# One alignment stage of an eight-part network: where the moves of the path are computed, and how its arrays travel

## The reference, cut to what matters

```python
def align_one(small, large):            # small: 77 x 256 context, large: 1024 x 256 normed tokens
    D = sqrt(max(|a|^2 + |b|^2 - 2 a.b, 0))       # 77 x 1024
    R = dtw_cost(D)     # R[i,j] = D[i,j] + min(R[i-1,j], R[i,j-1], R[i-1,j-1])
    # walk back from (76, 1023): at each cell take the least of diagonal, up, left
    # (in this order on a tie), until (0, 0)
    i_idx, j_idx, valid = backtrack(R)
    return zeros(1024, 256).at[j_idx].add(small[i_idx] * valid)
x = x + align(ctx, layernorm(x))
x = x + slots(layernorm(x))             # the stage behind it
```

## Time and the profile before

| | us |
|---|---|
| median of 3 runs | 4073.38 |
| lowest and highest | 4072.11, 4077.62 |
| the profiled execution, its own time | 4080.33 |
| its span, first to last instruction | 4078.5 |
| TensorE busy (share of the span) | 3017.4 (74%) |
| VectorE busy | 2092.9 (51%) |
| ScalarE busy | 1485.4 (36%) |
| GpSimd busy | 1015.0 (25%) |
| mean granted TensorE clock | 0.862 of full speed |

### The profile page before, as it was taken

How to read it: one execution, slowest core, us unless ns; L and a number is a source line. 1 busy time by engine, 2 the same in 40 slices (tenths; PEclk the granted TensorE clock), 3 DMA queues, 4 the chain that set the end, 5 groups by cost and what they waited for, 6 DMA issues and landing times. The chain is left out here.

```text
span 4078.5 us, 41019 instructions
## 1 busy us (share of the span) xinstructions
PE 3017.4 (74%) x14054; PEld 1775.1 (44%) x14054; DVE 2092.9 (51%) x3702; ACT 1485.4 (36%) x2034; POOL 1015.0 (25%) x593
## 2 busy tenths in 40 slices
PE   3999999999974577199567699998279520059979
PEld 1555555455534444189444333333279410024344
DVE  3655555565513354277454588776267444731270
ACT  2344444444433223256233255555156210012240
POOL 1355556565632211300311100000411312001100
PEclk7899999999986789599789699999589765579999
DMA  2000000000003300256100000000156224110050
GB/s 88 5 6 1 5 5 5 1 4 5 2 1 120 96 11 1 90 191 226 52 11 1 11 4 5 2 3 2 55 204 220 80 24 52 9 26 31 27 201 21
DMA packets 94303, 194.15 MB, mean 48 GB/s; under 512 B 30937, under 2 KB 67417, under 8 KB 86090
## 3 DMA queue, kind: packets, MB, share of 16 engines
q1 hardware_dynamic: 74730, 83.01, 7.6%
q0 software_dynamic: 16464, 103.18, 7.5%
q10 hardware_dynamic: 2960, 6.03, 0.4%
HBM read 149.16 MB, written 42.76 MB: 47 GB/s over the span
## 5 line engine op out<-in xcount | busy, mean ns | idle before, releaser
L602 POOL TENSOR_TENSOR A_key_sums<-A_key_sums,A_probs 128x1024 f32<-128x1024 f32 (+1 forms) x224 | 526.8, 2370 | 227.0 <-ACT A_probs L495 227.0
L495 ACT ACTIVATE A_probs<-A_banks 128x512 f32<-128x512 f32 (+1 forms) x576 | 329.4, 597 | 389.5 <-PE A_banks L415 387.1
L545 DVE TENSOR_REDUCE A_part_max<-A_banks 128x1 f32<-128x367 f32 x768 | 354.0, 530 | 156.9 <-PE A_banks L336 155.5
L1750 DVE TENSOR_REDUCE F_part_max<-F_banks 128x1 f32<-128x512 f32 x512 | 325.0, 683 | 59.6 <-PE F_banks L1603 56.8
L1696 ACT ACTIVATE F_probs<-F_banks 128x1024 f32<-128x1024 f32 x256 | 248.1, 1022 | 237.9 <-PE F_banks L1649 237.7
L364 PE MATMUL A_banks<-A_probs,A_v_tok 128*64 128x512 f32 x1152 | 278.7, 605 | 0.0
L413 PE MATMUL A_banks<-A_q_one,A_k_one 128*128 128x512 f32 (+1 forms) x576 | 258.3, 448 | 26.2 <-ACT A_probs L495 23.1
L336 PE MATMUL A_banks<-A_k_one,A_q_one 128*128 128x368 f32 x768 | 230.0, 382 | 6.8 <-ACT A_v_tok L475 6.4
L2064 PE MATMUL G_banks<-G_path,G_ctx_rows 77*128 77x512 f32 x16 | 14.0, 1071 | 293.9 <-DMA G_ctx_rows<-in_G_ctx_rows 293.9
L415 PE MATMUL A_banks<-A_q_two,A_k_two 128*128 128x512 f32 (+1 forms) x576 | 228.2, 396 | 0.0
L167 POOL TENSOR_SCALAR F_r<-F_r,F_ln_w 128x512 f32<-128x512 f32 x16 | 28.8, 1813 | 660.5 <-DVE F_r L132 660.5
(11 more groups left out here) (536 smaller groups left out, 6330.1 us busy)
## 6 DMA issues: line engine op xcount, KB each, us to landing
H_w<-in_H_w SPq DMA_DIRECT2D x11, 1024.0 KB, 4.8
moe_in<-A_zeros ACTq DMA_DIRECT2D x1, 5888.0 KB, 17.3
D_tile_in<-moe_in SPq DMA_DIRECT2D x23, 256.0 KB, 5.3
moe_out<-D_z SPq DMA_DIRECT2D x23, 256.0 KB, 4.9
F_tile_in<-moe_in SPq DMA_DIRECT2D x23, 256.0 KB, 5.2
moe_out<-F_z SPq DMA_DIRECT2D x23, 256.0 KB, 4.9
H_phi<-in_H_w SPq DMA_DIRECT2D x5, 1024.0 KB, 4.7
B_tile_in<-moe_in SPq DMA_DIRECT2D x15, 256.0 KB, 2.9
```

The lines of the kernel that those rows point to most:

```text
L495: act.activation(probs[0:kw, j, kt % RING, blk * BLK:(blk + 1) * BLK], ps[0:kw, half % 3, :], ACT.Exp, scale=1.0 / 8.0).then_inc(s["exp_re ...
L545: dve.tensor_reduce(part_max[:, i // 3, i % 3:i % 3 + 1], ps[:, MAX_BANKS[i % 3], 0:PIECE], AX.X, ALU.max).then_inc(s["piece_max"], 1)
L602: pool.tensor_tensor(key_sums[0:kw, j, :], before, probs[0:kw, j, kt % RING, :], ALU.add).then_inc(s["summed"], 1)
L1750: op = dve.tensor_reduce(part_max[:, maximum_at(hd, qt), kb:kb + 1], bank, AX.X, ALU.max)
```

## The change

The distances are stored and fetched for each sequence as soon as its two blocks are ready; each skewed fetch is cut in a first quarter of the slots (FIRST = 23) and the rest, with semaphores of their own. `G_start` is loaded early. Only `cost_dram` is padded, with a `fill` of 15 x 1024 in place of 15 x 4096. TensorE multiplies the context and the tokens ahead of the norm of the tokens.

Blocks G2 to G5 become one block. The totals stay in SBUF, and the moves are computed from them in the wave layout, [64, 92 x 64], by five VectorE instructions and two shuffles that fetch the neighbour lane's edge. The path is stored in two parts for each sequence (the later 46 slots, LATE, when they are done, the earlier 46 at the end) and loaded straight for each sequence. The context rows are loaded at the block's start and split in a rounded part and a rest, both fp32r, so each product in fp32 becomes two accumulating products in fp32r. GpSimd presets the path array and one slot of each move array.

```diff
-    def skewed(a, b):
-        return bass.AP(a.tensor, b * ROWS * S + PAD * W, [[S - W, CK], [S, SLOTS], [1, W]])
+    FIRST = SLOTS // 4
+    LATE = SLOTS // 2
+    def skewed(a, b, first=0, last=SLOTS):
+        return bass.AP(a.tensor, b * ROWS * S + PAD * W + first * S, [[S - W, CK], [S, last - first], [1, W]])
...
 # G1
-            pool.memset(fill[:, 0], BIG).then_inc(s["filled"], 1)
-            pool.memset(fill[:, 1], 0.0).then_inc(s["filled"], 1)
+                pool.memset(fill[:, :], BIG).then_inc(s["filled"], 1)
...
-            sp.wait_ge(s["cost_ready"], NBLK)
-            sp.dma_start(straight(cost_dram), cost[:, :].rearrange("r (b n) -> r b n", b=B)).then_inc(s["stored"], 16)
-            sp.wait_ge(s["stored"], count + 16)
+                sp.wait_ge(s["wave_filled"], 1)
+                sp.dma_start(total[:, 0, :], t["G_start"]).then_inc(start_loaded, 16)
+                sp.wait_ge(s["wave_filled"], 2)
+                sp.wait_ge(s["padded"], 16 * 2 * B)
+                for b in range(B):
+                    sp.wait_ge(s["cost_ready"], (b + 1) * NBLK // B)
+                    sp.dma_start(straight(cost_dram, b), cost[:, b * S:(b + 1) * S]).then_inc(s["stored"], 16)
+                    sp.wait_ge(s["stored"], 16 * (b + 1))
+                    lanes = slice(32 * b, 32 * b + CK)
+                    sp.dma_start(cost_wave[lanes, 0:FIRST], skewed(cost_dram, b, 0, FIRST)).then_inc(first_loaded, 16)
+                    sp.dma_start(cost_wave[lanes, FIRST:], skewed(cost_dram, b, FIRST)).then_inc(rest_loaded, 16)
 # one block for what were G2 to G5
+            move = sc.sb("move", [LANES, 2, SLOTS + 1, W + 1])
+            left = sc.sb("left", [LANES, SLOTS + 1, W + 1])
+            path = sc.sb("path", [LANES, SLOTS + 1, W + 1])
+            path_rows = sc.sb("path_rows", [CTX, B, S], F32R)
...
+            @block.sync
+            def _(sp):
+                sp.dma_start(ctx_rows[:, :, :], t["G_ctx_rows"]).then_inc(s["ctx_loaded"], 16)
+                sp.wait_ge(s["path_zeroed"], 1)
+                sp.dma_start(path[:, SLOTS, :], t["G_end"]).then_inc(s["end_loaded"], 16)
+                for first, last in ((LATE, SLOTS), (0, LATE)):
+                    sp.wait_ge(s["path_ready"], SLOTS - first)
+                    for b in range(B):
+                        sp.dma_start(skewed(path_dram, b, first, last), path[32 * b:32 * b + CK, first:last, 0:W])\
+                          .then_inc(path_stored[b], 16)
+                for b in range(B):
+                    sp.wait_ge(path_stored[b], 32)
+                    sp.dma_start(path_rows[:, b, :].bitcast(F32), straight(path_dram, b)).then_inc(path_loaded[b], 16)
+            @block.scalar
+            def _(act):
+                act.wait_ge(s["ctx_loaded"], 16)
+                act.activation(ctx_hi[:, :, :], ctx_rows[:, :, :], ACT.Copy).then_inc(s["hi_ready"], 1)
+            @block.vector
+            def _(dve):
+                dve.wait_ge(s["hi_ready"], 1)
+                dve.tensor_tensor(ctx_lo[:, :, :], ctx_rows[:, :, :], ctx_hi[:, :, :].bitcast(F32), ALU.subtract)\
+                   .then_inc(s["lo_ready"], 1)
+                dve.wait_ge(start_loaded, 16)
+                dve.wait_ge(first_loaded, 16 * B)
+                for n in range(SLOTS):
+                    if n == FIRST:
+                        dve.wait_ge(rest_loaded, 16 * B)
...                   # the three instructions of a slot as before
+                c_up, c_diag, c_left = total[:, 0:SLOTS, 1:], total[:, 0:SLOTS, 0:W], total[:, 1:, 0:W]
+                up, diag, to_left = move[:, 0, 0:SLOTS, 0:W], move[:, 1, 0:SLOTS, 0:W], left[:, 0:SLOTS, 0:W]
+                step(dve.tensor_tensor(least[:, :, :], c_up, c_left, ALU.min))
+                step(dve.tensor_tensor(diag, c_diag, least[:, :, :], ALU.is_le))
+                step(dve.tensor_tensor(up, c_up, c_left, ALU.is_le))
+                step(dve.scalar_tensor_tensor(out=to_left, in0=diag, scalar=0.0, in1=up, op0=ALU.is_equal, op1=ALU.is_gt))
+                step(dve.tensor_tensor(up, up, diag, ALU.is_gt))
+                step(dve.stream_shuffle(move[:, 1, 0:SLOTS, W], move[:, 1, 1:SLOTS + 1, 0], from_right))
+                step(dve.stream_shuffle(left[:, 0:SLOTS, W], left[:, 1:SLOTS + 1, 0], from_right))
...                   # 92 slots backward, four instructions each as before, then x + ps four times
+            @block.tensor
+            def _(pe):
+                pe.wait_ge(s["lo_ready"], 1)
+                for n in range(NBLK):
+                    b, blk = divmod(n, S // BLK)
+                    if blk == 0:
+                        pe.wait_ge(path_loaded[b], 16)
+                    for c in range(C):
+                        for k, part in enumerate((ctx_hi, ctx_lo)):
+                            mm = pe.matmul(ps[:, C * n + c, :], part[:, b, c * P:(c + 1) * P],
+                                           path_rows[:, b, blk * BLK:(blk + 1) * BLK], start=k == 0, stop=k == 1)
+                    mm.then_inc(s["out_ps"], 1)
```

More of the change, by code:

```diff
@@ L1823, in align_stage @@
[L1823 to L1843, removed]
-            pool.memset(fill[:, 0], BIG).then_inc(s["filled"], 1)
-            pool.memset(fill[:, 1], 0.0).then_inc(s["filled"], 1)
[L1846 to L1864, removed]
-                for c in range(C):
[L1866 to L1908, removed]
-            sp.wait_ge(s["cost_ready"], NBLK)
-            sp.dma_start(straight(cost_dram), cost[:, :].rearrange("r (b n) -> r b n", b=B)).then_inc(s["stored"], 16)
-            sp.wait_ge(s["stored"], count + 16)
@@ L1914, in align_stage @@
[L1914 to L1958, removed]
-        up = least
-        diag, left = (sc.sb(n, [CTX, B, S + 1]) for n in ("diag", "left"))
-        filled, back_filled, loaded, dve_step, stored = (
-            sc.sem(n) for n in "filled back_filled loaded dve_step stored".split())
-        block = stack.enter_context(nc.Block())
-        @block.gpsimd
-        def _(pool):
-            for a in (here, over):
-                pool.memset(a[:, :, 0:1], BIG).then_inc(filled, 1)
-            pool.memset(over[0:1, :, 1:], BIG).then_inc(filled, 1)
-            for a in (diag, left):
-                pool.memset(a[:, :, S:S + 1], 0.0).then_inc(filled, 1)
-            for a in (move[:, 0], move[:, 1], left_moves[:, :, :], path_wave[:, :, :]):
-                pool.memset(a, 0.0).then_inc(back_filled, 1)
-            pool.wait_ge(back_filled, 4)
-            pool.memset(move[:, 0, SLOTS, :], 1.0).then_inc(back_filled, 1)
-            pool.wait_ge(back_filled, 5)
-        @block.sync
-        def _(sp):
-            sp.dma_start(here[:, :, 1:], straight(total_dram)).then_inc(loaded, 16)
-            sp.dma_start(over[1:, :, 1:], straight(total_dram)[0:CTX - 1]).then_inc(loaded, 16)
-            sp.wait_ge(dve_step, 6)
-            for a, dst in ((up[:, :, 0:S], 0), (diag[:, :, 1:], 1), (left[:, :, 1:], 2)):
-                sp.dma_start(straight(move_dram[dst]), a).then_inc(stored, 16)
-            sp.wait_ge(stored, 48)
-        @block.vector
-        def _(dve):
-            step = chain(dve, dve_step)
-            dve.wait_ge(filled, 5)
-            dve.wait_ge(loaded, 32)
-            c_up, c_diag, c_left = over[:, :, 1:], over[:, :, 0:S], here[:, :, 0:S]
-            step(dve.tensor_tensor(least[:, :, :], c_up, c_left, ALU.min))
-            step(dve.tensor_tensor(diag[:, :, 0:S], c_diag, least[:, :, :], ALU.is_le))
-            step(dve.tensor_tensor(least[:, :, :], c_up, c_left, ALU.is_le))
-            step(dve.tensor_scalar(not_diag[:, :, :], diag[:, :, 0:S], -1.0, 1.0, ALU.mult, ALU.add))
-            step(dve.tensor_tensor(up[:, :, 0:S], least[:, :, :], not_diag[:, :, :], ALU.mult))
-            step(dve.tensor_tensor(left[:, :, 0:S], not_diag[:, :, :], up[:, :, 0:S], ALU.subtract))
@@ L2003, in align_stage @@
-    with ExitStack() as stack:
-        sc = Scope(nc, stack, "G4")
-        left, path = left_moves, path_wave
-        below = sc.sb("below", [LANES, 2, W])
-        enter = sc.sb("enter", [LANES, W])
-        loaded, edge_ready, below_ready, enter_ready, row_ready, stored = (
-            sc.sem(n) for n in "loaded edge_ready below_ready enter_ready row_ready stored".split())
-        from_right = [CK] + list(range(CK - 1)) + list(range(CK, 32))
-        block = stack.enter_context(nc.Block())
-        @block.sync
-        def _(sp):
-            for b in range(B):
-                for a, src in zip((move[:, 0], move[:, 1], left), move_dram):
-                    sp.dma_start(a[32 * b:32 * b + CK, 0:SLOTS], skewed(src, b)).then_inc(loaded, 16)
-            sp.dma_start(path[:, SLOTS, :], t["G_end"]).then_inc(loaded, 16)
-            sp.wait_ge(row_ready, SLOTS)
-            for b in range(B):
-                sp.dma_start(skewed(path_dram, b), path[32 * b:32 * b + CK, 0:SLOTS, 0:W]).then_inc(stored, 16)
-            sp.wait_ge(stored, 32)
-        @block.vector
-        def _(dve):
```

(42 more changed lines are left out.)

129 lines of the change are left out of this document (added).

## The result

The changed kernel takes 3998.33 us (median of 4 runs, 3996.7 to 4002.21) against 4072.74 (4 runs beside it): 74.4 us less, ratio 0.9817 with a 95% interval of 0.98 to 0.9834. The forecast was 4001.

The account below looks back on a forecast made before the run. One engine or transfer at a time was taken as the path, mostly transfer waits between passes. Savings 4.2 + 53.3 + 16.6 - 1.5 = 72.6 us from 4073.38 give 4001 us, range 3989 to 4013.

Parts of the forecast that it names:

- Middle: Between the forward and backward passes: transfers and waits go, five instructions and two shuffles come; 53.3 us sooner.
- the bounds: Between the passes, each shuffle of 92 columns: from 0.14 us if columns are free to 12.9 us; 0.25 taken.
- Head: First fill to forward pass: earlier distances and fetches by sequence, start waiting for context rows; 4.2 us sooner.
- Tail: Last backward scan to last add: half stores, loads by sequence and fp32r products; 16.6 us sooner.
- Backward pass: Backward slots: the first half's store runs under the last 46 slots without slowing them; 0 us.
- Given back: nH, behind the stage: less TensorE work in front leaves more of it at half clock; 1.5 us lost.
- The dearer moves: Rival, between the passes: shuffles cost by the column (+25 us) or runs of 64 at half rate (+31); 4026 to 4032; 10%.
- The head that isn't late: Rival, head: context rows land past the fetches at 3316, pass starts near 3317.3; 4.3 us better, 3997; 8%.
- The clock behind the stage: Rival, H stage products: the clock stays low, making the kernel slower than before; up to 4226 us; 3%.

Follow-up runs that it names:

- three runs: Changed kernel with context rows loaded first in G1, with each fetch uncut, and with both edits; heads 28.8, 32.9 and 32.0 us against 33.7.
- fetch_at_end: Changed kernel with both sequences' distances stored when all are ready, then both fetched, uncut; head 40.2 us against 33.7.
- the two uncut runs: Changed kernel with each sequence's fetch in one transfer, context rows loaded where the change put them or first in G1; heads 32.9 and 32.0 us.
- path_at_once: Changed kernel with each sequence's path stored in one transfer after the last slot; tail 21.3 us against 16.8.
- fp32_products: Changed kernel with the last products in fp32 from the context rows, copy and subtraction kept unused; tail 23.5 us against 16.8.
- warm_clock: Changed kernel with 21 extra TensorE products during the last backward slots and the path's store and load; tail 14.3 us, nH 22.3.
- moves_alone: Kernel before with only the moves computed in the wave layout, in one block; distances, path transfers and fp32 products as before; 4020.31 us, ratio 0.9869.
- no_cut: Changed kernel with each sequence's fetch in one transfer, not cut at slot 23; head 32.9 us against 33.7.
- pool_left: Changed kernel with left moves made by GpSimd beside the backward pass, using ScalarE's copy; middle 27.0 us against 32.8, backward pass 110.1 against 99.7.
- both_parts: Changed kernel with context rows loaded first in G1 and 21 extra TensorE products; 3986.14 us against 3998.78, ratio to the kernel before 0.9789.

## Why the prediction was right

The total is closer than its terms: the stretches saved 4.2 us more than forecast (76.8 against 72.6), nearly all of it in the head, while the runs moved by 74.4. That the time came out only 2.7 us from 4001 is in part luck.

**Middle: right in mechanism and size**, 52.9 against 53.3. Five instructions of 6.28 us (6.3 forecast), cut operands and all. The shuffles took 0.54 each, not 0.25: priced between the bounds at 1 ns a column, they cost 4.4 ns. That is 0.6 us in all. The prediction gives 1 ns for every other VectorE row, but the scan of the earlier trace rows took 0.34 us for 64 columns where the minimum beside it took 0.21: the rate is not the same for all. The Trainium skill's 2400 ns for 2048 columns ("VectorE: DVE Perf Modes", section on the perf-mode tier table) would be 1.2 ns a column; the measurement decides: 0.54 us for 92. Why the 92 columns here, 260 bytes apart, cost more wasn't tried.

**Head: right mechanism, the gain mis-sized by half**, 8.3 against 4.2. That the pass stands behind `ctx_rows`, and the cut at FIRST gives nothing, was forecast and shown by three runs. The 8.3 us are made up so: the last distances are stored 21.5 us after the first fill in place of 24.8, 3.3 sooner; copy and subtraction of the context add 1.5; storing and fetching by sequence brings the 6.5 of fetch_at_end. What the shorter fill and the earlier products each do of the 3.3 wasn't tried. The terms against the forecast, each from its own start: distances 1.2 sooner for sequence 0, since the clock rose along with TensorE's start and a little more (at 3281.9 against 3294.8, 5.1 us after the first product against 6.5); fetch of sequence 0 and store of sequence 1 7.5 us in place of 8.7; fetch of sequence 1 6.9 in place of 7.9; hand-overs 0.5. Together 3.9 of the 4.1 us. Most of the two middle ones has one cause, shown by fetch_at_end and the two uncut runs: I priced a fetch at 7.6, from a row in which two were in flight. (Two slips in the working changed nothing: half of 0.876 gives blocks of 3.50 us and not 3.43, and 3320.0 with its three terms gives 3321.5, a gain of 4.3.)

**Tail: right in mechanism and size**, 16.8 against 16.9: stores landed 4.0 and 6.4 us after the last scan (4.35 and 6.8 forecast), the first product came at 8.4, as forecast. path_at_once showed 4.5 us for the two parts of the store, fp32_products 6.7 for fp32r.

**Backward pass: right at nothing.** Stores under the slots didn't move 99.6.

**Given back: 1.1 against 1.5, right by luck.** The clock rose at 3534.4 in nH, 5.5 us into it against 3.4 before, and warm_clock shows what the low clock costs: at full clock nH takes 22.3. But the reason forecast, 7 us less work in front of nH, didn't hold: fp32_products has the 14 us of work and 25.4, moves_alone too and 24.8, and no_cut has the changed kernel's short tail and 24.2. In the ten profiles with a change and no extra products the rise comes 3.6 to 6.0 us into nH, without order by the work in front; what sets it in a run stays open.

**Rivals.** The dearer moves had 0.6 us of truth. The head that isn't late was ruled out by the waits in the changed profile: the first slot came 1.3 us after ScalarE had got the context rows, at 3308.67, 5 us after the first quarter. The clock behind the stage rose, 5.5 us into nH.

## What to carry to other kernels

A data layout that lets the next step read what the last one wrote can be worth more than anything done to the transfers: before, from the three stores to the last of the six skewed loads VectorE waited 45 us, more than the 31 of five whole-array instructions. When an edit puts a new load in front of an engine's list, ask what lies before it in its queue, and move a load that depends on nothing to where the queue is idle. Price a transfer from a row with the same company: alone, or with the next one in flight.

## What the runs showed of the hardware

- A GpSimd instruction that reads two operands in SBUF held up a VectorE instruction with two operands in SBUF until it ended: in pool_left 0.22 us became 4.04, and a scan of 0.34 became 4.05. GpSimd's presets, which read nothing, left such instructions at their length (before: 2.29 us beside a fill and without one), but not the one with a single operand, 5.50 us. That instruction ended 1.08 us after the fill of 5.13 (3426.07 to 3431.20), and not with it, as the prediction reads it. The same kind on 77x512 took 0.42 us, and beside a fill 1.23 before and 1.94 in the changed kernel, ending 0.3 after the fill both times. The Trainium skill ("SBUF — State Buffer", section "SBUF: two separate sides") has both cases; the traces agree.
- TensorE's granted clock fell from 1.0 to 0.5 some 0.7 us behind an idle gap of 2.4 us in both_parts, and held behind one of 2.3 us in warm_clock.
- A shuffle took 0.14 us for one column, and for columns 260 bytes apart 0.18 us for 8 (pool_left) and 0.54 for 92.
- The same instructions ahead of the alignment ended between 3272 and 3284 us in thirteen profiles. The changed kernel has 3275.0 and 3278.4, its variants 3272.4 to 3280.1, moves_alone 3275.2; the kernel before, profiled once, is the latest, 3283.9, and its profiled execution was 7 us over its median. A profile pair compares stretches, not totals.
